# Two attention layers over eight images: the next image's load is requested by ScalarE instead of SyncE, behind the copy of the high parts of the second group's keys

## The reference, cut to what matters

```python
# layer 0: 8 heads of 32 channels
mean = jnp.mean(x, axis=1, keepdims=True); var = jnp.var(x, axis=1, keepdims=True)
xn = (x - mean) / jnp.sqrt(var + EPS) * gamma
qkv = jnp.einsum('oc,bcn->bon', w_qkv, xf)
sim = jnp.einsum('bhdi,bhdj->bhij', q, k) * scale + bias[None]   # bias: an MLP of relative positions
attn = _stable_softmax(sim)
out = jnp.einsum('bhij,bhdj->bhdi', attn, v)
x = jnp.einsum('oc,bcn->bon', w_out, out) + residual
# layer 1: one head
f = Wf x + bf; g = Wg x + bg; hh = Wh x + bh
attn = jax.nn.softmax(jnp.einsum('bno,bom->bnm', f, g), axis=2)
x = gamma * jnp.einsum('bci,bij->bcj', hh, attn) + x
```

## Time and profile before

| | |
|---|---|
| Median of 3 runs | 1933.42 us (1932.26 to 1933.76) |
| The profiled execution | 1937.73 us |
| Its span, first to last instruction | 1935.6 us |
| TensorE busy | 1628.7 us (84%) |
| VectorE busy | 1508.7 us (78%) |
| ScalarE busy | 1388.3 us (72%) |
| GpSimd busy | 75.6 us (4%) |
| DMA | 122.46 MB, mean 63 GB/s over the span |
| Mean granted TensorE clock | 0.896 of full speed |

### The profile page before, as it was taken

The page is one execution under the profiler, slowest core; times in us unless marked ns, Lnnn a source line. Parts: engine busy times, 40 slices in busy tenths (PEclk is TensorE's granted clock), DMA queues, the critical chain, the costliest instruction groups (busy, mean ns, idle before and its releaser), DMA issues.

```text
span 1935.6 us, 18745 instructions
## 1 busy us (share of the span) xinstructions
PE 1628.7 (84%) x5969; PEld 764.5 (39%) x5969; DVE 1508.7 (78%) x2201; ACT 1388.3 (72%) x2043; POOL 75.6 (4%) x36
## 2 busy tenths in 40 slices
PE   6644889789996899969997899959997899989988
PEld 2121333434443354424434354423534344434424
DVE  5334789679896898869896898868896898999863
ACT  1133788668785788858885787857886688888853
POOL 1100100010000000010000100010000100000000
PEclk8566778989998899979998899979998899999999
DMA  1396022402034021512034020421034010330010
GB/s 55 60 218 170 1 55 77 131 1 55 1 121 109 1 55 49 149 33 55 1 99 131 1 55 23 141 66 47 10 99 131 1 55 11 121 78 1 1 44 22
DMA packets 59029, 122.46 MB, mean 63 GB/s; under 512 B 22506, under 2 KB 25130, under 8 KB 58922
## 3 DMA queue, kind: packets, MB, share of 16 engines
q1 hardware_dynamic: 58932, 121.28, 22.9%
HBM read 78.66 MB, written 44.13 MB: 63 GB/s over the span
## 4 chain that ended last, share of the span: by engine, by line
PE 46%; DVE 22%; issue 15%; DMA 8%; ACT 4%; SPq 3%; POOL 2%; DVEq 0%; POOLq 0%; ACTq 0%
DVE biased L1066 11%; PE psum L643 9%; PE psum L568 9%; PE psum L670 7%; DVE biased L1080 5%; PE psum L622 5%; DMA xn<-in_x_dram 4%; PE psum L623 3%; PE psum L446 3%; PE psum L491 3%; PE psum L460 2%; ACT biased L840 2%; DMA k_parts<-st 2%; PE psum L525 2%; PE psum L501 1%
## 5 line engine op out<-in xcount | busy, mean ns | idle before, releaser
L1066 DVE CUSTOM_DVE_ANT_0 biased<-psum,bias_lines_sb 128x1024 f32<-128x1024 f32 x512 | 617.1, 1221 | 253.7 <-PE psum L623 211.8
L840 ACT ACTIVATE biased<-biased,nmax 128x1024 f32<-128x1024 f32 x512 | 587.3, 1147 | 245.0 <-DVE nmax L1066 241.3
L1080 DVE TENSOR_TENSOR biased<-psum,bias_lines_sb 128x1024 f32<-128x1024 f32 x512 | 597.9, 1218 | 53.6 <-PE psum L643 39.6
L857 ACT ACTIVATE probs<-biased 128x1024 f32<-128x1024 f32 x512 | 536.3, 1056 | 142.9 <-DVE biased L1080 120.6
L643 PE MATMUL psum<-q_stack,k_stack 98*128 98x512 f32 x1024 | 400.2, 499 | 36.3 <-DVE nmax L1066 16.1
L622 PE MATMUL psum<-k_stack,q_stack 96*128 96x512 f32 x512 | 339.3, 663 | 94.2 <-DVE nmax L1066 52.7
L643 PEld LDWEIGHTS psum<-q_stack,k_stack 98*128 98x128 f32 x1024 | 182.7, 205 | 328.2 <-DVE biased L1080 153.9
L670 PE MATMUL psum<-probs,vT 128*32 128x512 f32 x2048 | 283.1, 623 | 6.1 <-DVE st L955 3.9
L622 PEld LDWEIGHTS psum<-k_stack,q_stack 96*128 96x128 f32 x512 | 103.5, 202 | 286.1 <-DVE nmax L1066 177.5
L623 PE MATMUL psum<-k_stack,q_stack 96*128 96x512 f32 x512 | 216.1, 422 | 0.0
L568 PE MATMUL psum<-probs 128*128 128x512 f32 x384 | 186.6, 592 | 0.0
(11 more groups left out here) (86 smaller groups left out, 1267.8 us busy)
## 6 DMA issues: line engine op xcount, KB each, us to landing
k_stack<-k_parts SPq DMA_DIRECT2D x48, 512.0 KB, 7.3
q_stack<-q_parts SPq DMA_DIRECT2D x96, 256.0 KB, 5.7
k_parts<-st SPq DMA_DIRECT2D x16, 1024.0 KB, 3.9
q_parts<-st SPq DMA_DIRECT2D x16, 1024.0 KB, 3.9
xn<-in_x_dram SPq DMA_DIRECT2D x8, 1024.0 KB, 11.2
x<-in_x_dram SPq DMA_DIRECT2D x8, 1024.0 KB, 9.2
out_dram<-x SPq DMA_DIRECT2D x8, 1024.0 KB, 4.1
bias_lines_sb<-bias_lines SPq DMA_DIRECT2D x32, 240.0 KB, 23.4
```

Source lines behind the costliest of these rows:

```text
L840: nc.scalar.activation(biased[:, m % BIASED, :], biased[:, m % BIASED, :], ACT.Exp, scale=-1.0, bias=nmax[:, m:m + 1], accum_out=rowsum[:, ...
L857: nc.scalar.activation(probs[:, n % P_SLOTS], biased[:, n % BIASED, :] .rearrange("p (i n) -> p i n", i=2), ACT.Exp).then_inc(SEMS["probs_ ...
L1066: nc.vector.tensor_tensor_reduce(biased[:, m % BIASED, :], pair(bank_of(g, first, ("rows", m))), bias_lines[:, g * HG + h, a0:a0 + N], -1. ...
L1080: nc.vector.tensor_tensor(biased[:, n % BIASED, :].rearrange("p (i n) -> p i n", i=2), psum[:, bank:bank + 2, :], bias_lines[:, g * HG + 2 ...
```

## The change

SyncE's request of the next image goes away together with its two waits, and ScalarE gets one directly behind `high_k`. The wait for `qk_mm` stands ahead of `high_k` already; the one for `v_mm` moves along. The transfer itself, its source, its target and its semaphore, stays the same, and so do the waits of `sum_x`.

```diff
@@ SyncE
                 k_out(b, 1)
                 k_in(b, 1)
-                if not last:
-
-                    need(sp, "v_mm", b, NT)
-                    need(sp, "qk_mm", b, split(1, 1))
-                    sp.dma_start(xn[:], x_dram[b + 1]).then_inc(x_loaded, 16)
                 for r in range(NHALF):
                     shift_to_stack(b, 0, r)
@@ ScalarE
                     need(act, "qk_mm", b, split(1, 1))
                     need(act, "q_stored", b, 16 * G)
                     nc.scalar.activation(st[:, 0, :], pair(6), ACT.Copy).then_inc(SEMS["hi_ready"], 1)
+                    if not last:
+                        need(act, "v_mm", b, NT)
+                        nc.scalar.dma_start(xn[:], x_dram[b + 1]).then_inc(x_loaded, 16)
```

## The result

The changed kernel takes 1855.38 us (median of 4 runs, 1853.92 to 1856.88), the kernel before 1933.59 us beside it (4 runs, 1932.26 to 1936.24). The ratio is 0.9594, interval 0.9577 to 0.9611: 78 us faster. A second set of runs gave 0.9598 (0.9583 to 0.9613).

A forecast was written before the change was run, and what follows sets the result against it. The late load of `xn` was taken to bound each batch, stalling TensorE at `sum_x`. Six batches at 10.3 + 1.7 = 12.0 us plus 9.9 for the first gave 82 us: 1933.4 - 82 = 1851 us, range 1833 to 1872.

The forecast's parts named there:

- The range of the forecast itself: 1840 to 1862 us: 7 x 1 us for the low clock, 3 us for ScalarE, 2.5 for the first batch.
- The request moves forward: Fifth batch: the request for `xn` goes from 1039.65 to about 1031.5, 8.1 us earlier, ahead of the keys' store and loads.
- What the load meets: Behind the rest of the queries' loads, `xn` lands at 1037 to 1038 instead of 1050.76, in the fifth batch.
- What `sum_x` waits for: The keys' store, landing at 1039.2 (1038.3 to 1040.8); TensorE's 10.3 us wait goes, at worst all but 0.2 us.
- The clock: TensorE stays at full clock without the stall, so `centre` starts 2.7 us after `mean` instead of 4.40: 1.7 us gained.
- ScalarE's cost: The 0.4 us request fits into a 0.50 us gap on ScalarE: cost 0, otherwise 7 x 0.4 = 3 us.
- GpSimd beside VectorE: `sum_x` now runs while VectorE works, but just misses the shift's small operations, which end at 1038.25: cost 0.
- collision: Rival, chance 7%: `sum_x` meets the shift on VectorE, costing 2.1 us, seven times 15 us; 1866 to 1881 us.
- The first batch: The keys' store lands up to 2.5 us later, at 172.05; `mean` starts at 174.5 instead of 184.41, gaining 9.9 us.
- From the profiled execution to the median: The profiled execution lay 4.3 us above the median; the same 82 us taken off the median 1933.4 gives 1851.
- The second way: Last batch, without a next image, as model: stall to columns phase takes 18.5 us instead of 30.7, gaining 12.2 per batch.

The follow-up runs named there:

- the run with SyncE's early request: Changed kernel, but SyncE instead of ScalarE requests the next image, ahead of its store of the second group's keys: 1856.51 us, ratio 0.9603.
- The run with the small load: Changed kernel, but the load brings 64 KB of the next image instead of 1 MB: 1851.81 us, ratio 0.9572.
- the run with the request behind the store: Changed kernel, but SyncE requests the next image, directly behind its keys' store request and ahead of the keys' loads: 1876.73 us, ratio 0.9702.
- two matmuls: Kernel with SyncE's request between keys' store and loads, plus two matmuls of known weights before TensorE's wait for `sum_x`: 1866.99 us, ratio 0.9658.
- the same cure: Kernel before, with nine matmuls of known weights in TensorE's 10 us wait for `sum_x`: 1937.23 us against 1937.39, ratio 1.0005.
- the fivefold dose: Changed kernel with four more requests of 8 KB copies on ScalarE right behind that of the next image: 1856.69 us, ratio 0.9586.

## Why the prediction was right

The forecast was 1851 us (1833 to 1872); measured 1855.4. The gain was forecast as 82 us and measured as 78 between medians and 82.0 between the two profiled executions; this last match is in part luck, as told below. The range of the forecast itself, 1840 to 1862, is a little narrower than the terms named for it, which add up to 12.5 us on either side.

- *The request moves forward.* Right, and more than forecast. It went out at 980.49, 5.0 us ahead of the store's request instead of 2.9, and 1 us before `high_k`, behind which it is written, began (981.54). In six of the seven batches it went out 0.8 to 1.1 us before that copy began, and in the first with its start. So "directly behind `high_k`", and that an engine takes its instructions strictly in order, hold for the order of issue only.
- *What the load meets.* The landing was right, its length was not: 8.1 us after the request (7.3 to 8.8) where I gave 5 to 7. From 980 to 984 nothing of `xn` moved and the queries' loads took all (SyncE's queue had a share of 106.5%, that is all of the engines); from 984 to 989 all 272 packets of it did. It came through as the earlier requests ran out, as I had assumed, and not by turns; only from 984 to 985 did both queues move data (shares of 65.3% and 41.0%). It landed where forecast, near 988.6, which is 1037.5 on the scale of the kernel before.
- *What `sum_x` waits for.* The store, as forecast. It landed 6.0 us after its request in the fifth batch and 4.8 to 6.4 in the batches from the second on: between the value I took (4.8) and the worst bound (6.4). I had most of `xn` through by 1035.3; in fact the engines moved `xn` alone from 985 to 987, while the store stood requested since 985.45. That TensorE was covered even so is partly luck: in the seventh batch it waited 0.3 us, and in the sixth batch of the run with SyncE's early request 0.6 us, which cost 2 us with the clock. The run with the small load shows that the late store cost next to nothing from the second batch on (0.1 us a batch), and the run with the request behind the store shows what lies just beyond: 3 us a batch.
- *The clock.* 10.3 + 1.7 = 12.0 us a batch were forecast, 12.1 measured. The wait was 10.4 us in the mean of the six batches, and `centre` starts 2.8 us after `mean` where it was 4.4, so the clock's term is 1.6. That this is the clock's is shown where the wait is short (1.4 to 1.6 us a batch, by two matmuls). In the kernel before, the same cure gave 1.1 us locally and nothing in the end.
- *ScalarE's cost.* 0, shown by the fivefold dose. The gap of 0.50 us was not even needed: the request went out while an exponential ran.
- *GpSimd beside VectorE.* `sum_x` starts at 991.53, 2.2 us behind the shift's last operation (989.30), and 1.0 us behind it in the closest batch. No collision; the tile work beside it kept its 1.22 us.
- *The first batch.* 8.6 us from the store's request to `sum_x` (21.2 to 12.7) where I had 9.9, since the store landed 12.6 us after its request and not 11.4.
- *From the profiled execution to the median.* Here the forecast was off by 4 us: 82 from the waits of one execution, 78 between the medians (75 to 82 by the interval). The profiled execution of before lay 4.3 us above its median, that of after 0.35 above its own. 2.1 us of the 82.1 between the two spans had arisen before the first place that the change touches (the first store request at 160.69 before, 158.58 after), so they are no part of the change, and 80 are left. Where the other 2 lie was not found.
- *The second way*, by the last batch, gave 12.2 us a batch and is as good as the first. It put the stretch from the stall to the columns phase at 18.5 us; in the fifth batch it took 18.0 (993.72 to 1011.75).

## What to carry to other kernels

When the load of the next piece stands behind a store that must land and behind loads that nobody needs soon, move its request ahead of them. Which engine's queue it went to mattered nothing once it stood early; at the old time the second queue gave some 13 of the 78 us. Look at how far it must move: behind the store it lost a quarter of the gain, since a wait of 1.8 us cost nearly as much again by the clock. A step that is only just covered in the batch that you read may not be in another: look at all of them. And a profiled execution is one draw from the runs, so a gain added up from its waits can be some us off that of the medians.

## What the runs showed of the hardware that I had not expected

- In the changed kernel's fifth batch a transfer requested on ScalarE's queue went out 1.05 us before the copy that stands ahead of it began, while the exponential before that was running.
- A wait of 0.63 us of TensorE was followed by 3 us at half clock (sixth batch of the run with SyncE's early request); one of 0.29 us left it at full (seventh batch of the changed kernel).
- Two transfers of 1 MB, a store and a load, requested 0.47 us apart on one queue, fell to 213 to 246 GB/s for a while, where a store alone moves at 418. With the load first (requested 5.5 us ahead, in the run with SyncE's early request), they moved at 401 to 434 GB/s from 984.5 to 988.5.
- Next to 1.5 MB of the keys' loads on the other queue, 96% of `xn` had moved 8 us after its request, and its landing came at 11.1 us.
- A load on ScalarE's queue moved nothing for 3.5 us while SyncE's earlier requests took all engines, and then all of its 272 packets in the next 5 us.
